# GpSimd's adds over nine tap planes, joined into one of 2352 elements, with every ninth product of the first 15 tiles summed there

## What is computed

```python
x = x + _L0_conv_ref(_gn(x), ...)   # sign, depthwise 3x3, prelu, bn, sign, 1x1, prelu, bn, plus residual
x = x + _L1_conv_ref(_gn(x), W, b)

def _L1_conv_ref(x, W, b):          # involution: a 3x3 filter of its own for every pixel and channel
    filters = jnp.einsum('bchw,oc->bohw', x, W) + b[None, :, None, None]
    filters = filters.reshape(B, C, K * K, H, Wd).transpose(0, 1, 3, 4, 2)
    patches = _extract_patches(x)
    return jnp.sum(patches * filters, axis=-1)
```

## Time and profile before

| | |
|---|---|
| median of 3 executions | 744.23 us (743.96 to 745.69) |
| the profiled execution, its time | 744.98 us |
| span of the profile | 743.1 us |
| busy: DVE, POOL, ACT, PE | 677.6, 623.0, 491.1, 618.1 us |

### The profile page before, as it was taken

The page is one execution under the profiler, slowest core; times in us unless marked ns, Lnnn a source line. Parts: engine busy times, 40 slices in busy tenths (PEclk is TensorE's granted clock), DMA queues, the critical chain, the costliest instruction groups (busy, mean ns, idle before and its releaser), DMA issues.

```text
span 743.1 us, 18722 instructions
## 1 busy us (share of the span) xinstructions
PE 618.1 (83%) x8001; PEld 254.2 (34%) x8001; DVE 677.6 (91%) x999; ACT 491.1 (66%) x612; POOL 623.0 (84%) x423
## 2 busy tenths in 40 slices
PE   3549779898888889888888989898898888888887
PEld 1324334243333434233333424333243423332213
DVE  4939879999999999999999999999999999999995
ACT  6857795868677685877678586867858586724200
POOL 2005678998998989899898999899899899989996
PEclk9769999999999999999999999999999999999999
DMA  5136496979989797979979797998979788987985
GB/s 211 69 132 117 81 265 150 230 175 235 214 182 267 159 255 155 255 171 212 260 158 265 158 243 172 225 231 174 266 159 247 153 191 168 189 185 158 204 174 140
DMA packets 34279, 142.10 MB, mean 191 GB/s; under 512 B 3348, under 2 KB 11540, under 8 KB 32276
## 3 DMA queue, kind: packets, MB, share of 16 engines
q0 software_dynamic: 17232, 75.87, 55.7%
q1 hardware_dynamic: 16940, 65.03, 25.8%
q10 hardware_dynamic: 24, 0.00, 0.0%
HBM read 26.03 MB, written 25.69 MB: 70 GB/s over the span
## 4 chain that ended last, share of the span: by engine, by line
POOL 69%; issue 10%; DVE 7%; ACT 6%; PE 5%; DMA 1%; SPq 0%; POOLq 0%; ACTq 0%; DVEq 0%
POOL ob L388 14%; POOL prod L373 13%; POOL prod L379 13%; POOL prod L366 8%; POOL prod L346 7%; POOL prod L355 7%; DVE prod L871 5%; POOL prod L358 5%; PE tap_ps L454 3%; POOL st L333 2%; ACT unused L545 2%; ACT ab L545 2%; PE dw_ps L463 1%; POOL st L331 1%; PE dw_ps L489 1%
## 5 line engine op out<-in xcount | busy, mean ns | idle before, releaser
L454 PE MATMUL tap_ps<-q,w_t 64*64 64x392 f32 x2304 | 481.1, 506 | 42.2 <-DVE prod L871 17.1
L871 DVE SCALAR_TENSOR_TENSOR prod<-tap_ps,bias,q 128x784 f32<-128x784 f32 x478 | 473.4, 1028 | 27.3 <-PE tap_ps L454 25.1
L454 PE MATMUL tap_ps<-mirror,w_t 64*64 64x392 f32 x2304 | 474.7, 506 | 0.0
L454 PEld LDWEIGHTS tap_ps<-q,w_t 64*64 64x64 f32 x2304 | 148.6, 133 | 258.1 <-DVE prod L871 178.6
L545 ACT ACTIVATE ab<-dw_ps,col 128x784 bf16<-128x784 f32 x124 | 116.9, 992 | 41.2 <-PE dw_ps L489 41.2
L388 POOL TENSOR_TENSOR ob<-prod 128x784 f32<-128x784 f32 x63 | 142.0, 2254 | 0.2 <-POOL prod L379 0.2
L373 POOL TENSOR_TENSOR prod<-prod 128x784 f32<-128x784 f32 x63 | 139.3, 2211 | 1.0 <-DMA prod<-prod 0.9
L454 PEld LDWEIGHTS tap_ps<-mirror,w_t 64*64 64x64 f32 x2304 | 135.9, 133 | 1.1 <-issue 1.1
L379 POOL TENSOR_TENSOR prod<-prod 128x784 f32<-128x784 f32 x63 | 134.1, 2129 | 0.0
L489 PE MATMUL dw_ps<-signs,dw_diag 64*64 64x392 bf16 x2232 | 130.5, 335 | 4.3 <-ACT ab L545 2.2
L346 POOL DMA_DIRECT2D prod<-prod x63 | 78.9, 1253 | 64.6 <-DVE prod L871 64.6
(11 more groups left out here) (119 smaller groups left out, 432.6 us busy)
## 6 DMA issues: line engine op xcount, KB each, us to landing
prod<-prod POOLq DMA_DIRECT2D x63, 1176.0 KB, 10.4
out_dram<-ob SPq DMA_DIRECT2D x31, 784.0 KB, 9.4
xb<-in_x_dram SPq DMA_DIRECT2D x15, 1568.0 KB, 9.1
mirror<-q SPq DMA_DIRECT2D x64, 203.0 KB, 4.0
xb<-in_x_dram SPq DMA_DIRECT2D x2, 784.0 KB, 5.8
out_dram<-ob SPq DMA_DIRECT2D x2, 392.0 KB, 2.3
prod<-in_L_conv_W_dram SPq DMA_DIRECT2D x1, 288.0 KB
prod<-in_L_conv_pw_weight_dram SPq DMA_DIRECT2D x1, 32.0 KB
```

Of the source, the lines that this page charges most:

```text
L454: mm = pe.matmul(rows3(tap_ps[to, slot, side, 0:CH]), w_t[own, k, :], moving, start=True, stop=True)
L871: v.scalar_tensor_tensor(place.rearrange("p j (a b) -> p j a b", b=WD), psum.rearrange("p j (a b) -> p j a b", b=WD), s_(t, B4) if k == 4 ...
```

## The change

POOL's adds are joined. In the first 15 tiles all quarters now go the way of the odd ones (POOLED holds all four): no `pair` on DVE, one add_mean on ACT per quarter. POOL then makes three instructions per quarter: add_wide, planes 3 to 5 += planes 6 to 8 (2352 elements), add35, plane 3 += 5, and final, ob = 3 + 4. The three quarters of the last tile that POOL sums keep the pair on DVE and have add_early (6 += 7), add_wide over two planes (3, 4 += 5, 6; 1568 elements), and final. The delays are new, and the tables for the tile's and the first tiles' steps move by a few units (two of their lines are shown).

```diff
         def on_pool(g):
-            return g % 2 == 1 and g < (TILES - 1) * QUARTERS
+            return g % QUARTERS in POOLED and g < (TILES - 1) * QUARTERS
...
-            def add67(t, qq):
+            def add_early(t, qq):
                 g = quarter(t, qq)
                 pr = planes(g)
 
-                if on_pool(g):
-                    pool.wait_ge(prod_done, KK * g + 8)
-                    pool.tensor_tensor(pr[6], pr[6], pr[7], ALU.add).then_inc(summed67_first, 1)
-                else:
+                if not on_pool(g):
                     pool.wait_ge(paired, kept(g))
                     pool.tensor_tensor(pr[6], pr[6], pr[7], ALU.add).then_inc(summed67, 1)
 
-            def add68(t, qq):
+            def add_wide(t, qq):
+                g = quarter(t, qq)
+                pr = prod[:, g % BUFS, :, :]
+
+                pool.wait_ge(folded[g % BUFS], 16 * (g // BUFS + 1))
+                if on_pool(g):
+                    pool.wait_ge(mean_added, pooled(g))
+                    pool.tensor_tensor(pr[:, 3:6, :], pr[:, 3:6, :], pr[:, 6:9, :], ALU.add).then_inc(summed_wide, 1)
+                else:
+                    pool.wait_ge(summed67, kept(g))
+                    pool.tensor_tensor(pr[:, 3:5, :], pr[:, 3:5, :], pr[:, 5:7, :], ALU.add).then_inc(summed_wide, 1)
+
+            def add35(t, qq):
                 g = quarter(t, qq)
                 pr = planes(g)
                 if on_pool(g):
-                    pool.wait_ge(summed67_first, pooled(g))
-                    pool.wait_ge(mean_added, pooled(g))
-                    pool.tensor_tensor(pr[6], pr[6], pr[8], ALU.add).then_inc(summed67, 1)
-
-            def add45(t, qq):
-                g = quarter(t, qq)
-                pr = planes(g)
-
-                pool.wait_ge(folded[g % BUFS], 16 * (g // BUFS + 1))
-                pool.tensor_tensor(pr[4], pr[4], pr[5], ALU.add).then_inc(summed45, 1)
-
-            def add36(t, qq):
-                g = quarter(t, qq)
-                pr = planes(g)
-                pool.wait_ge(summed67, g + 1)
-                pool.tensor_tensor(pr[3], pr[3], pr[6], ALU.add).then_inc(summed36, 1)
+                    pool.wait_ge(summed_wide, g + 1)
+                    pool.tensor_tensor(pr[3], pr[3], pr[5], ALU.add).then_inc(summed35, 1)
 
             def final(t, qq):
 
                 g = quarter(t, qq)
                 pr = planes(g)
                 wait(pool, stored[qq // 2], t.count(16))
-                pool.wait_ge(summed45, g + 1)
-                pool.wait_ge(summed36, g + 1)
+                if on_pool(g):
+                    pool.wait_ge(summed35, pooled(g))
+                else:
+                    pool.wait_ge(summed_wide, g + 1)
                 pool.tensor_tensor(ob[:, qq, :], pr[3], pr[4], ALU.add).then_inc(summed, 1)
...
- 'rstd0': -62,
- 'scales0': -61,
+ 'rstd0': -65,
+ 'scales0': -60,
...
-PW_DELAY = 5
+PW_DELAY = 6
...
-FOLD_DELAY = 6
-ADD67_DELAY = 12
-ADD68_DELAY = 15
-MEAN_DELAY = 11
-ADD45_DELAY = 17
-ADD36_DELAY = 20
+FOLD_DELAY = 4
+EARLY_ADD_DELAY = 14
+MEAN_DELAY = 12
+WIDE_ADD_DELAY = 20
+LATE_ADD_DELAY = 25
+POOLED = 0, 1, 2, 3
+
 OUT_DELAY = 25
```

More of the change, by code:

```diff
@@ L143, in preact_involution_kernel @@
         taps_ready, prod_done = sem("taps_ready"), sem("prod_done")
-        summed67, summed45, summed36, summed = sem("summed67"), sem("summed45"), sem("summed36"), sem("summed")
+        summed67, summed_wide, summed35, summed = sem("summed67"), sem("summed_wide"), sem("summed35"), sem("summed")
         folded, paired = [sem(f"folded{i}") for i in range(BUFS)], sem("paired")
-        mean_added, summed67_first = sem("mean_added"), sem("summed67_first")
+        mean_added = sem("mean_added")
         stored = [sem("stored0"), sem("stored1")]
@@ L347, in fold @@
                                max_dma_last_dim=6 * QP).then_inc(folded[g % BUFS], 16)
-            def add67(t, qq):
+            def add_early(t, qq):
+                g = quarter(t, qq)
+                pr = planes(g)
+                if not on_pool(g):
+                    pool.wait_ge(paired, kept(g))
+                    pool.tensor_tensor(pr[6], pr[6], pr[7], ALU.add).then_inc(summed67, 1)
+            def add_wide(t, qq):
+                g = quarter(t, qq)
+                pr = prod[:, g % BUFS, :, :]
[7 more added lines that the diff above has]
+            def add35(t, qq):
                 g = quarter(t, qq)
@@ L353, in add67 @@
                 if on_pool(g):
-                    pool.wait_ge(prod_done, KK * g + 8)
-                    pool.tensor_tensor(pr[6], pr[6], pr[7], ALU.add).then_inc(summed67_first, 1)
-                else:
-                    pool.wait_ge(paired, kept(g))
-                    pool.tensor_tensor(pr[6], pr[6], pr[7], ALU.add).then_inc(summed67, 1)
-            def add68(t, qq):
-                g = quarter(t, qq)
-                pr = planes(g)
-                if on_pool(g):
-                    pool.wait_ge(summed67_first, pooled(g))
-                    pool.wait_ge(mean_added, pooled(g))
-                    pool.tensor_tensor(pr[6], pr[6], pr[8], ALU.add).then_inc(summed67, 1)
-            def add45(t, qq):
-                g = quarter(t, qq)
-                pr = planes(g)
-                pool.wait_ge(folded[g % BUFS], 16 * (g // BUFS + 1))
-                pool.tensor_tensor(pr[4], pr[4], pr[5], ALU.add).then_inc(summed45, 1)
-            def add36(t, qq):
-                g = quarter(t, qq)
-                pr = planes(g)
-                pool.wait_ge(summed67, g + 1)
-                pool.tensor_tensor(pr[3], pr[3], pr[6], ALU.add).then_inc(summed36, 1)
+                    pool.wait_ge(summed_wide, g + 1)
+                    pool.tensor_tensor(pr[3], pr[3], pr[5], ALU.add).then_inc(summed35, 1)
             def final(t, qq):
@@ L385, in final @@
                 wait(pool, stored[qq // 2], t.count(16))
-                pool.wait_ge(summed45, g + 1)
-                pool.wait_ge(summed36, g + 1)
+                if on_pool(g):
+                    pool.wait_ge(summed35, pooled(g))
+                else:
+                    pool.wait_ge(summed_wide, g + 1)
                 pool.tensor_tensor(ob[:, qq, :], pr[3], pr[4], ALU.add).then_inc(summed, 1)
             for g in units:
-                for what, delay in ((fold, FOLD_DELAY), (add67, ADD67_DELAY), (add68, ADD68_DELAY), (add45, ADD45_DELAY),
-                                    (add36, ADD36_DELAY), (final, OUT_DELAY)):
+                for what, delay in ((fold, FOLD_DELAY), (add_early, EARLY_ADD_DELAY), (add_wide, WIDE_ADD_DELAY),
+                                    (add35, LATE_ADD_DELAY), (final, OUT_DELAY)):
                     for t, qq in quarters(g, delay):
@@ L934 @@
  'var0': -63,
- 'rstd0': -62,
- 'scales0': -61,
- 'inv_z': -57,
+ 'rstd0': -65,
+ 'scales0': -60,
+ 'inv_z': -55,
  'ratio': -55,
@@ L940 @@
  'job1': -46,
- 'job2': -32,
+ 'job2': -31,
  'job3': -25,
@@ L947 @@
  'rstd1': -12,
- 'q0': -11,
+ 'q0': -10,
  'q1': -9,
- 'inverse': -9,
+ 'inverse': -8,
 }
@@ L956 @@
      'square0': -67,
-     'var0': -66,
+     'var0': -67,
      'rstd0': -66,
@@ L964 @@
      'job2': -59,
-     'job3': -56,
+     'job3': -58,
      'sum1': -48,
@@ L971 @@
      'q0': -44,
-     'q1': -44,
+     'q1': -43,
      'inverse': -44},
- 1: {'sum0': -101,
+ 1: {'sum0': -100,
      'mean0': -100,
@@ L980 @@
      'scales0': -78,
[L981 to L984, removed]
+     'inv_z': -36,
+     'ratio': -35,
+     'job0': -37,
+     'job1': -31,
      'job2': -24,
@@ L989 @@
      'square1': -9,
-     'var1': -8,
+     'var1': -9,
      'rstd1': -8,
@@ L993 @@
      'q1': -7,
-     'inverse': -5},
+     'inverse': -4},
  2: {'sum0': -60,
@@ L997 @@
      'sign0': -58,
[L998 to L1001, removed]
+     'square0': -53,
+     'var0': -48,
+     'rstd0': -50,
+     'scales0': -46,
      'inv_z': -46,
@@ L1006 @@
      'job2': -31,
-     'job3': -24},
+     'job3': -25},
 }
 PROLOGUE = {
-    'bias': -50,
- 'turn_w': -46,
+    'bias': -49,
+ 'turn_w': -43,
  'copy_w': -45,
  'signs_rest': -43,
- 'square_0': -56,
+ 'square_0': -58,
  'square_1': -53,
- 'square_2': -50,
+ 'square_2': -52,
  'square_3': -47,
```

## The result

The changed kernel takes 749.49 us (median of 4, 749.21 to 750.0) against 744.51 for the kernel before on the same chip: 1.0068 times as long, 95% interval 1.0052 to 1.0084. The forecast was 750.4, slower, within 736 to 762.

What follows compares the result with a forecast made beforehand. DVE with its small waits bounds the kernel now; POOL would after the change. The middle's +1.5 and the tail's +4.7 make +6.2 on a median of 744.2: 750.4 us, range 736 to 762.

Steps and rivals of the forecast that it cites:

- Who bounds: Middle tiles: POOL takes over the pace from DVE, 42.8 us per tile against DVE's 40.7.
- The two add_mean more per tile on ACT: ACT's added work, about 1 us each beside 31.0 busy of 42.6, priced at nothing.
- The price of POOL's quarter: First 15 tiles: add_wide, fold, add35 and final take 10.19 us per quarter, 42.8 per tile with two rstd pairs.
- The joined add: add_wide of 2352 elements on POOL: 5.10 us, between 4.83 and 5.43, where three single adds take 5.43.
- fixed part: Cost of a POOL instruction regardless of size, saved twice by joining three adds: taken as 0.16 us, at most 0.30.
- The wait on the own engine: POOL's final waits for add35 right before it: 2.30 recorded plus 0.17 gap, exposing the fold's lag each quarter.
- The middle: From the fold of quarter 6 to that of quarter 59, 13.25 tiles: 567.1 us instead of 565.6, +1.5.
- The tail: Last tile, after the fold of quarter 59: DVE's products wait for POOL's finals, +4.7 us.
- the next gates: Last tile: finals of quarters 58 and 59, which DVE's products need, come 10.2 and 12.0 us later in turn.
- The start: First tiles, up to the fold of quarter 6: they hang on their statistics, so it stays at 128.78 us.
- DVE's waits at k = 3: Middle tiles: DVE waits for POOL's final at product k = 3, some 0.5 us in most quarters.
- the late chain: Rival, chance 0.07: rstd behind add_wide and fold delays q and next products; 1 us per tile exposed adds 13, some 763.

## Why the prediction was right

- **Who bounds.** POOL became the bound, as said: its idle time at the folds is gone past the first tiles, undoing the ninth products in the even quarters brings 6 us back, and making POOL's quarter longer by some 0.28 costs 13.6 us. The two add_mean more per tile on ACT, priced at nothing, cost nothing that shows: POOL never waits for ACT.
- **The price of POOL's quarter.** Predicted 10.19 and 42.8 per tile, measured 10.2 and 42.86. The joined add, chosen at 5.10 between 4.83 and 5.43, is 5.11 to 5.17. That the choice came out so near is partly luck: the rows gave only the two bounds, and by the forecast's own sum a fixed part of 0.25 in place of 0.16 would have turned the sign. With the 1.81 of 784 elements the measured 5.14 makes 2.12 ns per element (3.33 over 1568). The estimate from the Trainium skill's figure for 2048 elements (GPSIMD Engine Reference, Performance versus the Vector engine) was 2.09, and the trace agrees nearly.
- **The wait on the own engine.** Predicted 2.47 from add35 to final, measured 2.42 to 2.46 in the quarters of the tile above without an rstd pair between. Its two parts show apart in the experiments: lag of 0.45, gap of 0.07 to 0.14.
- **The middle.** Predicted +1.5, measured +2.4, a mere 0.07 us per tile off.
- **The tail.** Predicted +4.7, measured +4.7, and the steps fit too: k = 3 of quarter 60 comes 5.2 after fold 59 (5.3 predicted), the next gates 10.15 and 11.94 later (10.2 and 12.0), and k = 3 of quarter 63 another 9.7 (9.45). The profile puts the wait at quarter 60 down to TensorE, but the product starts 0.04 after the end of the final that it needs (699.87), as the next two do.
- **The start.** This is the term that was off most: I kept 128.78 for the fold of quarter 6, and it came at 126.77. One profile of each kernel is little to explain 2 us with; in the seven experiments that keep the changed kernel's order of POOL it lies between 125.5 and 128.7. What moves it stays open. That the total came within 1.1 us is partly luck: this miss of -2.0 hid the 0.9 that the middle was too low.
- DVE's waits at k = 3 are 0.8 us in 36 places rather than 0.5 in most quarters, about the same sum. Its busy time fell by 25.7 rather than 30. Products in a row start 0.945 apart, so 30 pairs are 28.4 of the union; the rest wasn't traced.
- Of the rivals, the late chain needs a note: it didn't happen here, but in the kernel with single adds in the order of before, the places of rstd alone were worth 21 us.

## What to carry to other kernels

Where two engines are within some per cent of each other, moving an operation from one to the other can change the owner of the pace, and then the gain on the first counts nothing: price the second one's period in full, from start to start, with the lag that its DMAs leave and with every wait for the instruction right before. Joining adds saved little here (some 0.28 us of 5.43), and the chain of dependent ones lost the overlap that separate ones had. And move the small operations that others wait for along with the large ones. Read the end of the program by itself: equal totals can hide a gain in the middle and a loss there.

## What the runs showed that was not expected

- Two one-element pairs of rstd per tile, one add later in POOL's queue, cost 20.8 us of 777.6.
- Three quarters on POOL should have run at 41.4 by both engines' sums, and the two profiled executions ran at 42.3 and 42.0; with uneven stretches smoothed the waits moved to another engine, and the time stayed.
- In the first of them the long tiles are those in which TensorE had stood still for 2.00 to 2.86 us and its granted clock had then fallen; with the change itself such tiles are no longer than the others.
- The accumulating fold takes 10.2 us (median) from issue to landing, which cost 23 us of waits as soon as its reader came that close behind it.
